# Attention over eight images: the next image's keys, queries and values move ahead of the last query chunk

## The reference, cut to what matters

```
x  = mean of 2x2 blocks                       # 8 x 64 x 64 x 64
tg = tok(gap * x)                             # gap: mean of x over the image, per channel
xK = sigmoid(tg @ Wq.T + bq) * (tg @ Wk.T + bk) + tg
y0 = branch(5x1 depthwise taps down the image) # taps, GELU, 64x64 product, scale
y1 = branch(1x5 depthwise taps along the rows)
xQ = tok(Wh @ [y0, y1] + bh)
xV = tok(x) @ Wo.T + bo
attn = softmax(xQ @ xK.T / 8)
z  = (attn @ xV) @ Wp.T + bp + xV
zn = layernorm(z)                             # then upsampled, then the second stage
```

## Time and profile before

| | us |
|---|---|
| Median of 3 runs (12581.31 to 12587.69) | 12582.6 |
| The profiled execution's own time | 12589.15 |
| Its span | 12587.3 |
| First stage, until the second stage's first instructions | about 4914 |
| Mean granted TensorE clock, share of full | 0.97 |
| Busy: PE 91%, DVE 79%, ACT 63%, POOL 63% | |

### The profile page before, as it was taken

The page is one execution under the profiler, slowest core; times in us unless marked ns, Lnnn a source line. Parts: engine busy times, 40 slices in busy tenths (PEclk is TensorE's granted clock), DMA queues, the critical chain, the costliest instruction groups (busy, mean ns, idle before and its releaser), DMA issues.

```text
span 12587.3 us, 161054 instructions
## 1 busy us (share of the span) xinstructions
PE 11479.8 (91%) x33595; PEld 4292.2 (34%) x33771; DVE 9913.6 (79%) x12698; ACT 7890.3 (63%) x12822; POOL 7875.4 (63%) x5926
## 2 busy tenths in 40 slices
PE   4989898989999998999999999999999999999998
PEld 1333333333333333333333333333333333333333
DVE  6454545454645444999999999999999999999999
ACT  1333333333333334888888888888888888888887
POOL 6030303030303002999999999999999999999999
PEclk9989898989999999999999999999999999999999
DMA  2010101010000001444444444444444444444444
GB/s 58 2 28 2 29 2 28 2 29 9 21 9 21 2 2 73 177 173 183 168 183 172 178 179 171 183 168 182 176 174 180 170 183 171 179 177 174 183 167 183
DMA packets 408439, 1433.35 MB, mean 114 GB/s; under 512 B 180242, under 2 KB 180370, under 8 KB 267926
## 3 DMA queue, kind: packets, MB, share of 16 engines
q1 hardware_dynamic: 408342, 1432.48, 30.6%
HBM read 1380.68 MB, written 51.62 MB: 114 GB/s over the span
## 4 chain that ended last, share of the span: by engine, by line
PE 16%; DVE 16%; issue 14%; ACT 12%; POOL 2%; DVEq 1%; ACTq 0%; POOLq 0%; DMA 0%; SPq 0%
DVE bbank L940 7%; PE ybank L1195 6%; DVE h L961 6%; ACT da L1085 4%; PE ubank L1137 2%; POOL e L837 2%; PE bbank L1185 2%; ACT L1018 2%; PE vbank L1144 2%; PE vbank L1143 2%; DVE qn L930 1%; PE ubank L1147 1%; ACT so L1053 1%; DVE dl L919 1%; ACT ed L1037 1%
## 5 line engine op out<-in xcount | busy, mean ns | idle before, releaser
L871 POOL TENSOR_TENSOR pr<-h,cc 128x512 f32<-128x512 f32 x4110 | 5170.0, 1272 | 647.8 <-DVE h L961 587.8
L961 DVE TENSOR_TENSOR_SCAN h<-da,h,bbank 128x512 f32<-128x512 f32 x3597 | 4506.4, 1264 | 0.0
L1195 PE MATMUL ybank<-pr,m_small 128*128 128x512 f32 x8214 | 4191.9, 602 | 0.3 <-POOL pr L871 0.3
L433 ACT ACTIVATE prob<-st 128x512 f32<-128x512 f32 x2048 | 1223.2, 597 | 2575.3 <-PE st L565 2575.3
L1085 ACT ACTIVATE da<-dl,a 128x512 f32<-128x512 f32 x3600 | 2445.1, 713 | 103.8 <-DVE dl L919 94.2
L940 DVE TENSOR_TENSOR bbank<-bbank,du 128x512 f32<-128x512 f32 x3598 | 2425.9, 674 | 60.5 <-PE bbank L1185 58.3
L308 DVE TENSOR_REDUCE mpart<-s 128x1 f32<-128x512 f32 x2048 | 1322.5, 686 | 1090.5 <-PE s L531 1082.4
L565 PE MATMUL st<-qf,kf 65*128 (+1 forms) x4096 | 2121.7, 620 | 5.9 <-ACT qf L437 5.9
L241 POOL TENSOR_TENSOR rowsum<-xin 128x1024 f32<-128x1024 f32 x64 | 153.9, 2405 | 2997.8 <-PE vb L598 2907.7
L1185 PE MATMUL bbank<-bcs,selb 96*128 96x512 bf16 x3599 | 1394.3, 388 | 545.1 <-DVE h L961 544.4
L1195 PEld LDWEIGHTS ybank<-pr,m_small 128*128 128x128 f32 x8214 | 1561.9, 194 | 907.7 <-issue 619.7
(11 more groups left out here) (156 smaller groups left out, 12444.9 us busy)
## 6 DMA issues: line engine op xcount, KB each, us to landing
cc<-c_rows SPq DMA_DIRECT2D x1032, 1024.0 KB, 7.7
cc<-c_rows SPq DMA_DIRECT2D x258, 512.0 KB, 11.5
upw<-up SPq DMA_DIRECT2D x260, 256.0 KB, 10.3
xin<-x SPq DMA_DIRECT2D x128, 512.0 KB, 6.8
out<-ot SPq DMA_DIRECT2D x256, 128.0 KB, 2.3
zw<-zn_tokens SPq DMA_DIRECT2D x780, 32.0 KB, 10.5
c_rows<-crows SPq DMA_DIRECT2D x258, 36.0 KB
zn_tokens<-znb SPq DMA_DIRECT2D x64, 128.0 KB, 2.0
```

Of the source, the lines that this page charges most:

```text
L433: act.activation(prob[t % 4][:, :], st[t % 2][:, :], ACT.Exp).then_inc(exp_done, 1)
L871: pool.tensor_tensor(pr[:, n % 8, :], h[:, n, :], cc[par][:, n, :], ALU.mult).then_inc(prod_done, 1)
L961: dve.tensor_tensor_scan(h[:, n, :], decay, inp, h[:, n, TB - 1:TB], ALU.mult, ALU.add).then_inc(scan_done, 1)
L1195: pe.matmul(ybank[:, :], w("ident"), pr[:, n % 8, :], start=False, stop=(n == S - 1))\
```

## The change

Keys and queries of image b + 1 are made between chunks 6 and 7 of image b, and chunk 7 carries the row maxima of the next image's chunk 0. For this the scaled image and the keys share one buffer `kt`, which exists twice, as do the values `vv`; the last chunk's queries have buffers `qlast` of their own. ACT's scaling of image b + 1 is spread over chunks 2 to 5 (`scaled`, two pieces at the end of each). On DVE the mean moves behind `normalise` of chunk 0, and the vertical taps to two pieces after chunks 1, 2 and 3 and one after 4 and 5. `normalise` of chunk 7 moves behind the maxima of the next image's chunk 1. SP's and POOL's programs keep their order; only one more memset is added. The key is formed in place: the scaled image stands in `kt` until L380 adds it to its product there. The constant table is loaded only up to the attention's part, and the loop over images is written out by twos.

```diff
@@ DVE @@
-                maxima(b * NQ)
+            def batch(b, p, first, more):
+
                 maxima(b * NQ + 1)
+                if not first:
+                    normalise(b - 1, 1 - p, NQ - 1)
+                taps = {1: (0, 1), 2: (2, 3), 3: (4, 5), 4: (6,), 5: (7,)}
+                for j in range(NQ - 2):
+                    maxima(b * NQ + j + 2)
+                    normalise(b, p, j)
+                    if more and j == 0:
+                        mean(b + 1)
+                    if more:
+                        for ch in taps.get(j, ()):
+                            vertical(b + 1, ch)
                 if more:
-                    mean(b + 1)
-                    vertical(b + 1, 0)
...
+                    keys_queries(b + 1, 1 - p)
+                    maxima(b * NQ + NQ)
+                normalise(b, p, NQ - 2)
@@ ACT @@
+            def batch(b, p, first, more):
+
+                g = b * NQ
+                exps(g, qf[64:65, TB:2 * TB], not first)
                 outputs(g)
+                exps(g + 1, qf[64:65, 2 * TB:3 * TB], True)
+                outputs(g + 1)
+                if more:
+                    act.wait_ge(gap_v, (b + 1) * 3 + 3)
+                with act.Fori(2, NQ - 2) as j:
+                    exps(b * NQ + j, qf[64:65, bass.ds((j + 1) * TB, TB)], True)
+                    outputs(b * NQ + j)
+                    if more:
+                        for half in range(2):
+                            scaled(1 - p, j * 2 + (half - 4))
+                exps(g + NQ - 2, qlast[p][64:65, :], True)
+                outputs(g + NQ - 2)
+                if more:
+                    keys_queries(b + 1, 1 - p)
+                    act.wait_ge(qm_done, (b + 2) * NQ)
+                exps(g + NQ - 1, qf[64:65, 0:TB] if more else None, True)
+                outputs(g + NQ - 1)
@@ PE @@
+                if fresh is not None:
+                    pe.wait_ge(sig_done, fresh * NQ + NQ)
                 for t in range(KT + 2):
...
+                    if fresh is not None and t == 1:
+                        pe.wait_ge(qm_done, fresh * NQ + NQ)
+                        pe.wait_ge(krow, fresh + 1)
+                        pe.wait_ge(v_done, fresh * NQ + NQ)
+                    first = 0 if fresh is None else 2
+                    if ahead is not None and first <= t < KT // 2 + first:
+                        for u in (2 * (t - first), 2 * (t - first) + 1):
+                            maxima_blocks(g + 1, ahead, u)
...
+            def batch(b, p, first, more):
+
+                g = b * NQ
+                chunk(g, p, qf[0:C + 1, 0:TB], TB, not first)
                 with pe.Fori(1, NQ - 1) as j:
-                    chunk(b * NQ + j, j, True, True)
-                chunk(b * NQ + NQ - 1, NQ - 1, False, True)
-                project(b * NQ + NQ - 1)
+                    chunk(b * NQ + j, p, qf[0:C + 1, bass.ds(j * TB, TB)], j * TB + TB, True)
+                if more:
+                    keys_queries(b + 1, 1 - p)
+                chunk(g + NQ - 1, p, qlast[p][0:C + 1, :], 0 if more else None, True, b + 1 if more else None)
```

More of the change, by code:

```diff
@@ L92, in attention_phase @@
         yg = sb("yg", [P, N])
[L93 to L95 removed]
+        kt = [sb(f"kt{i}", [P, N]) for i in range(2)]
+        qf = sb("qf", [P, N - TB])
+        qlast = [sb(f"qlast{i}", [P, TB]) for i in range(2)]
         ka = sb("ka", [P, N], BF16)
@@ L98, in attention_phase @@
         qm = sb("qm", [P, N], BF16)
-        v = sb("v", [P, KT, 2 * C])
+        vv = [sb(f"vv{i}", [P, KT, 2 * C]) for i in range(2)]
         sg = [sb(f"sg{i}", [P, TB]) for i in range(2)]
@@ L226, in _ @@
             pool.memset(xb[:, :], 0.0).then_inc(zeroed, 1)
-            pool.memset(v[:, :, 2 * C - 1:2 * C], 1.0).then_inc(zeroed, 1)
-            pool.wait_ge(zeroed, 3)
+            for i in range(2):
+                pool.memset(vv[i][:, :, 2 * C - 1:2 * C], 1.0).then_inc(zeroed, 1)
+            pool.wait_ge(zeroed, 4)
             with pool.Fori(0, B) as b:
@@ L414, in _, with exps @@
                 vertical(0, ch)
-            with dve.Fori(0, B - 1) as b:
-                image(b, True)
-            image(B - 1, False)
+            keys_queries(0, 0)
+            maxima(0)
+            batch(0, 0, True, True)
+            with dve.Fori(0, (B - 2) // 2) as b2:
+                for s in range(2):
+                    batch(b2 * 2 + s + 1, 1 - s, False, True)
+            batch(B - 1, 1, False, False)
+            normalise(B - 1, 1, NQ - 1)
         @block.scalar
         def _(act):
-            def exps(g, next_cols, rest):
+            def exps(g, next_row, rest, at=MAX_ROW_T):
                 for t in range(KT):
-                    if t == MAX_ROW_T and next_cols is not None:
-                        max_row(g + 1, next_cols)
+                    if t == at and next_row is not None:
+                        max_row(g + 1, next_row)
                     if t == KT - 6 and rest:
@@ new lines, in _ @@
+            act.wait_ge(small_in, 16)
+            act.wait_ge(gap_v, 3)
+            for ch in range(NQ):
+                scaled(0, ch)
+            keys_queries(0, 0)
+            act.wait_ge(qm_done, NQ)
+            max_row(0, qf[64:65, 0:TB])
+            batch(0, 0, True, True)
+            with act.Fori(0, (B - 2) // 2) as b2:
+                for s in range(2):
+                    batch(b2 * 2 + s + 1, 1 - s, False, True)
+            batch(B - 1, 1, False, False)
+            rstds(B * NQ - 1)
@@ L553, in project, with chunk @@
                 mm.then_inc(zt_mm, 1)
-            def chunk(g, j, ahead, behind):
+            def chunk(g, p, q, ahead, behind, fresh=None):
                 pe.wait_ge(mrow_done, g + 1)
-                q = qf[0:C + 1, bass.ds(j * TB, TB)]
+                if fresh is not None:
+                    pe.wait_ge(sig_done, fresh * NQ + NQ)
                 for t in range(KT + 2):
```

135 lines of the change are left out of this document (58 added, 77 removed), and 2 rows, old and new, of the table LAYOUT.

## The result

The changed kernel takes **12504.9 us** (median of four runs, 12496.9 to 12515.5) against 12583.9 us for the kernel before beside it: a ratio of 0.9937, 95% interval 0.9920 to 0.9955, so 79 us or 0.6% faster. The profiled execution took 12507.2 us, 82.0 less than the 12589.2 of the profiled execution before. Predicted were 12591 us, no change; the time lies in the range, but the sign was missed by more than a measurement is uncertain.

A forecast was written before the change was run, and what follows sets the result against it. ACT's `max_row`, once per chunk, was taken as the clock of the 4914 us before the second stage. Terms -158 - 110 + 25 + 251 = +8 us on 12582.6 gave 12591 us, range 12450 to 12640.

The forecast's parts named there:

- seam: From chunk 6's `max_row` to that of the next image's chunk 1: 22.6 us shorter, seven times, -158 us.
- late DVE goes: Chunk 2's maxima no longer wait behind the mean and first vertical taps: 15.8 us saved, seven times, -110 us.
- scaling: After chunks 2 to 5, ACT's added scalings delay an exponential that PE needs: 0.9 us, 28 times, +25 us.
- POOL and DVE meet: POOL's taps hold six DVE instructions of `normalise`, delaying chunk 3's maxima in images 1 to 6: 41.9 us each, +251 us.
- the phase: POOL's taps start 57.2 us after the `normalise` that releases the load ends; DVE's next L338 starts at 60.3 us.
- K = 57: Time in us of the keys and queries between chunks 6 and 7, two of eight pieces at the upper clock.
- F: Extra time in chunk 7 after the keys, for first tiles at the lower clock: 2 us, between 0 and 2.9.
- the clock stays up in the keys: Rival: PE keeps the upper clock from a dense chunk through the keys, 13 us less seven times, 12500 us; chance 0.12.
- The rival ending slower, with POOL out of step: POOL's taps start 2.9 us later or over 4 us earlier than assumed against L338: 12608 or 12621 us; chance 0.22.

The follow-up runs named there:

- experiment 4: Also `early_table`: the changed kernel with ACT's sigmoid table loaded before `outputs` of chunk 6, ahead of the copy of `osb`; 12431.7 us, ratio 0.9878 to the kernel before.
- experiment 6: The kernel before with only the mean and vertical taps at the places they have in the change; 12478.9 us, ratio 0.9912.
- `combined`: The changed kernel with normalisation parameters in PSUM, key products over 128 rows, sigmoid table loaded earlier and scalings spread behind four tiles; 12202.4 us, ratio 0.9696.

## Why the prediction was wrong

Term by term, in us, from the intervals of the two profiled executions:

| term | predicted | measured |
|---|---|---|
| seam | -158 | -192.5 |
| late DVE goes | -110 | -109.4 |
| scaling | +25 | +22 |
| POOL and DVE meet | +251 | +195.9 |
| branch back | none | +8.8 |
| start of image 0 and second stage | 0 | -6.7 |
| sum | +8 | -82 |

The mechanisms were right in the main: the seam with its shorter stages, the late DVE, the meeting at chunk 1 to 2 in images 1 to 6 and not in image 0, and the places of both. That the measured time still lies in the range is owed to the width of the range, not to the sum. The sum was one of large terms of both signs (-268 and +276), and two were mis-sized in the same direction.

- **The step that failed most is in "POOL and DVE meet elsewhere": "then they pass at the ends of POOL's product, product, addition, product, addition and product".** It gave one POOL instruction to each of six DVE instructions. The measured ends are at five: POOL's addition starts 0.08 us after the product before it ends, and there a 0.3 us instruction passes without a hold (that the addition's wait for the product makes this gap is read from the rows). That is 8.9 us of each 41.9, 53 of the 55 us by which this term was off. What was decided rightly there: that L338 (now L344) is held at all, that L354 and L357 are not, and the phase to 0.6 us.
- **In the seam, "I take the first two of eight pieces at that, worth 3 us: K = 57" failed.** It treated the clock as one course for all images. It was two: with F, the keys cost 44.6 us where the clock stayed up (seams of 106.8 and 107.0 less 62.3) and 58.8 where it fell early (121.1), the latter close to the 57 + 2 of the sum. Two of seven stayed up, two more fell later (117.0 and 119.5), and that is the 34 us. The rival "the clock stays up in the keys" had a price of 13 us an image, and the measured difference is 14; what the sum needed was this price times a share. Which keys would keep the clock could not be had from the rows, and differs between runs. Its counter-argument, 0.50 under 98% busy in the earlier trace rows, came from keys that start at the lower clock; experiment 4 shows that from the upper clock those same 64 rows keep it, if PE doesn't stop.
- **The branch back (+8.8) was missed** since no row of the kernel before has it at a place where PE is the bound: there the loop over images ends at the seam, where PE waits 8 us for ACT in any case. That it is hidden there is argued, not shown.
- The late DVE (-110) and scaling (+25, 0.9 each against 0.8) were right, the first also by itself in experiment 6 (-110).
- The rival ending slower, with POOL out of step, did not come: the first L344 started between 1.5 and 3.7 us after POOL's first product in all six images, and no phase brought in a further POOL instruction.

The chances followed from a sum of which no term was doubted on one side. A forecast of no change that rests on 276 us against 268 is a forecast of the small difference, and both unmeasured terms had been set near their costly ends.

## What to carry to other kernels

Where two engines lock a port, count the holds by the other engine's instructions and look at which of them wait on each other: a short instruction slips through such a gap, and an operand moved to PSUM took the hold away from all the instructions of `normalise` (-179 us here). Before anything is reordered to hide a stage in which PE is busy, read its granted clock: adding zero rows to the small products gave -129 us in the kernel before, more than the reordering with all its parts. Where the clock hangs on a short stop, look for the instruction of another engine at its head: loading a table one copy earlier gave -73 us. And where a seam is moved, look for what it drags along: a load that comes one chunk later met another engine's work there and gave back most of what the seam had gained.

## What the hardware showed that was not expected

- With PE 98% busy on products over 64 rows the granted clock stayed at 0.50 for 42 us; with 128 rows it was at 1.00 after 5 us. From 1.00, 64 rows kept it for all products of the keys where PE had no stop (seven of seven, `early_table`), and lost it in 19 of 24 behind a stop of 0.87 us (four runs).
- A branch back over the loop body of two images stopped PE for 2.5 to 3.0 us, and made the interval 4.3 to 4.7 us longer with the clock behind it (the change and `combined`); unrolled, both stops were gone.
- The second stage has two durations some 22 us apart, in kernels in which it is the same code. The short one goes with 155 to 160 us at the lower clock, the long one with 221 to 244; why the clock differs is open.
